# Gate and up products of two token blocks as seven block products instead of eight

## The reference

```python
g = jnp.einsum('bsd,edf->ebsf', h, Wg)          # e = 8 experts, d = 256, f = 1024
u = jnp.einsum('bsd,edf->ebsf', h, Wu)
expert_outs = jnp.einsum('ebsf,efd->ebsd', silu(g) * u, Wd)
expert_output = jnp.einsum('be,ebsd->bsd', gating_probs, expert_outs)
shared = jnp.einsum('bsf,fd->bsd', silu(h @ Sg) * (h @ Su), Sd)
return (1.0 - sg) * expert_output + sg * shared
```

## Time and profile before

| | |
|---|---|
| runs | 1375.63, 1377.25, 1380.95 us |
| profiled execution | span 1373.0 us; what lies around the span is not listed apart, the median of the runs is 4.25 us above the span |
| mean granted TensorE clock | 0.992 |
| busy in the span | PE 1346.5 us (98%), VectorE 755.6 (55%), ScalarE 329.8 (24%), GpSimd 45.7 (3%) |
| matmuls | 5832, of them 9 x 576 = 5184 in the experts and 384 in the GELU network |
| DMA | 39.6 MB, 29 GB/s over the span |

### The profile page before, as it was taken

One profiled execution on the slowest core, in us unless ns is written; L12 is line 12 of the kernel. 1 busy time (PEld: TensorE's weight loads), 2 busy tenths in 40 slices (PEclk: granted clock), 3 DMA queues, 4 the chain that ended last, 5 costly groups with the idle time before them and its releaser, 6 DMA issues.

```text
span 1373.0 us, 16497 instructions
## 1 busy us (share of the span) xinstructions
PE 1346.5 (98%) x5832; PEld 1079.9 (79%) x5832; DVE 755.6 (55%) x1231; ACT 329.8 (24%) x565; POOL 45.7 (3%) x48
## 2 busy tenths in 40 slices
PE   6799999999999999999999999999999999999998
PEld 4568888888888888888888888888888888888886
DVE  6956555555555555555555555555555555554444
ACT  2555622211112222111122221121222211111111
POOL 7500000000000000000000000000000000000000
PEclk8899999999999999999999999999999999999999
DMA  8020200000000000000000000000000000000000
GB/s 249 15 92 9 84 23 23 23 23 23 23 23 23 23 23 23 23 23 23 23 23 23 23 23 23 23 23 23 23 23 23 23 23 0 0 0 1 26 19 15
DMA packets 16432, 39.59 MB, mean 29 GB/s; under 512 B 6562, under 2 KB 9122, under 8 KB 16290
## 3 DMA queue, kind: packets, MB, share of 16 engines
q1 hardware_dynamic: 15536, 39.39, 8.8%
q10 hardware_dynamic: 882, 0.02, 0.0%
HBM read 37.31 MB, written 2.10 MB: 29 GB/s over the span
## 4 chain that ended last, share of the span: by engine, by line
PE 96%; DVE 3%; DMA 1%; ACT 0%; issue 0%; SPq 0%; DVEq 0%; ACTq 0%
PE ps L858 96%; DMA xT<-in_x_rows 1%; DVE x_dn L683 0%; DVE w_lo L713 0%; DVE gate L570 0%; DVE xT L609 0%; DVE poly L602 0%; DVE row_max L644 0%; DVE xT L729 0%; PE ps L875 0%; DVE denom L664 0%; DVE x_lo L721 0%; DVE x_dn L658 0%; DVE nb_all L595 0%; DVEq L45 0%
## 5 line engine op out<-in xcount | busy, mean ns | idle before, releaser
L858 PE MATMUL ps<-x_hi,w_hi 128*128 (+1 forms) x1216 | 480.7, 395 | 2.8 <-DVE x_lo L721 2.7
L858 PE MATMUL ps<-x_lo,w_hi 128*128 (+1 forms) x1216 | 480.7, 395 | 0.0
L858 PE MATMUL ps<-x_hi,w_lo 128*128 (+1 forms) x1216 | 477.4, 393 | 0.0
L828 DVE SCALAR_TENSOR_TENSOR hidden<-stage,gate,ps 128x512 f32<-128x512 f32 x288 | 215.3, 748 | 440.6 <-ACT stage L516 440.6
L516 ACT ACTIVATE stage<-ps 128x512 f32<-128x512 f32 x288 | 172.2, 598 | 928.3 <-PE ps L858 928.2
L858 PEld LDWEIGHTS ps<-x_hi,w_hi 128*128 128x128 f32 x1216 | 228.1, 188 | 60.1 <-issue 2.9
L858 PEld LDWEIGHTS ps<-x_hi,w_lo 128*128 128x128 f32 x1216 | 228.5, 188 | 54.3
L858 PEld LDWEIGHTS ps<-x_lo,w_hi 128*128 128x128 f32 x1216 | 228.2, 188 | 52.1
L858 PE MATMUL ps<-h_hi,w_hi 128*128 128x512 f32 x640 | 252.3, 394 | 0.0
L858 PE MATMUL ps<-h_lo,w_hi 128*128 128x512 f32 x640 | 251.9, 394 | 0.0
L858 PE MATMUL ps<-h_hi,w_lo 128*128 128x512 f32 x640 | 251.2, 392 | 0.0
(11 more groups left out here) (105 smaller groups left out, 286.2 us busy)
## 6 DMA issues: line engine op xcount, KB each, us to landing
raw<-in_moe_w SPq DMA_DIRECT2D x36, 768.0 KB, 4.3
out_x<-xT SPq DMA_DIRECT2D x8, 256.0 KB, 2.4
xT<-in_x_rows SPq DMA_DIRECT2D x2, 528.0 KB, 4.8
x_up<-in_x_rows SPq DMA_DIRECT2D x2, 520.0 KB, 6.6
x_dn<-in_x_rows SPq DMA_DIRECT2D x2, 520.0 KB, 10.0
raw<-in_fc_w SPq DMA_DIRECT2D x1, 1024.0 KB, 10.7
x_up<-in_x_rows SPq DMA_DIRECT2D x2, 504.0 KB, 9.3
x_dn<-in_x_rows SPq DMA_DIRECT2D x2, 504.0 KB, 11.8
```

What stands on the lines that cost most here:

```text
L828: nc.vector.scalar_tensor_tensor(hidden[:, k % PAIR, :], stage[:, k % PAIR, :], gate[:, ds(e, 1), ds(tb, 1)].rearrange("p e t -> p (e t)") ...
L858: return nc.tensor.matmul(out_ap, lhsT, rhs, start=first, stop=last)
```

## The change

A group is now one hidden chunk k and one round p of two token blocks (512 columns each). Gate and up for both blocks are the 2x2 block product of A = [[gate c0, gate c1], [up c0, up c1]] and B = [[x c0 of block 0, x c0 of block 1], [x c1 of block 0, x c1 of block 1]]. It is made in Winograd's form with seven block products. The sums S1 to S4 of weights (four 128x128 subtractions or additions a chunk, VectorE) and T1 to T4 of tokens (once, before the experts) are new. Down products stay as they were (four a group). PE issues 11 products of three matmuls a group: 33.

Partial sums are shared through PSUM. A11*B11 goes to bank A. ScalarE copies bank A into bank B (`seed`, PSUM to PSUM) and PE adds A12*B21 to A (gate of block 0) and S2*T2 to B. VectorE adds bank B and a ScalarE copy of S1*T1 (bank E, `p5_out`) and writes the sum back into bank E (`gate1_seed`), on which PE adds S4*B22 (gate of block 1). S3*T3 is added to B, VectorE sums B and the copy to the up of block 1 (`up1_sum`), and A22*T4 is added to B for the up of block 0. Bank B alternates between 6 and 7; the four down sums hold banks 0 to 3.

The gate value is applied once a round when the down sums are added to `xT`, and no longer to each hidden chunk. Both high parts of the hidden chunks are made on ScalarE. The weights come as 72 pieces (one chunk of one expert, six 128x128 blocks) through a ring of four raw slots; split weights lie in eight tiles, one per chunk, used by both rounds. The last three tiles take the place of the GELU network's weights. The experts are: the first written out, a loop over 1 to 7 with 16 groups in its body, the last written out. In the diff below the first `expert` is ScalarE's stream, the second VectorE's, and `group` is TensorE's.

```diff
+        A21, A11, A12, A22, D0, D1, S1, S2, S3, S4 = range(RT)
+        B11, B21, B22, T4, T1, T2, T3 = range(XT)
+        ROUNDS = 2
+        GROUPS = ROUNDS * FC
...
             with sp.Fori(1, E) as e:
-                for q in range(NT):
-                    sp.wait_ge(wlo_done, (e - 1) * (NT * PIECES) + (q + 1) * PIECES)
-                    sp.dma_start(raw[:, q * WQ:(q + 1) * WQ],
-                                 moe_w[ds(e, 1), :, q * WQ:(q + 1) * WQ].rearrange("e p w -> (e p) w")) \
-                      .then_inc(raw_in[q], 16)
+                for k in range(FC):
+                    sp.wait_ge(wlo_done, e * FC + k - RAWS + 1)
+                    piece_load(e, k)
...
+            def piece_high(e, k, after_round=True):
+                q = e * FC + k
+                act.wait_ge(wsum_done, 4 * q + 4)
+                if after_round:
+                    act.wait_ge(down0_done, (e - 1) * GROUPS + FC + k + 1)
+                nc.scalar.activation(w_hi[k][:, :, :], piece[:, k % RAWS, A11:RT, :], ACT.Copy).then_inc(whi_done, 1)
...
+            def seed(e, i):
+                n = e * GROUPS + i
+                act.wait_ge(p1_ps, n + 1)
+                if not starts(e, i, 2):
+                    act.wait_ge(hidden0_done, n - 1)
+                nc.scalar.activation(ps[:, BANK_B + i % 2, :], ps[:, BANK_A, :], ACT.Copy).then_inc(seeded, 1)
...
+            def expert(e, first, last):
+                for i in range(GROUPS):
+                    before = not starts(e, i, 1)
+                    seed(e, i)
+                    if before:
+                        hidden1_high(*earlier(e, i, 1))
+                    p5_out(e, i)
+                    gate0(e, i)
+                    if before:
+                        hidden0_high(*earlier(e, i, 1))
+                    gate1(e, i)
...
+                    elif i in (2, 3):
+                        piece_high(e, i + 4)
+                    elif i >= FC + 2 and not last:
+                        piece_high(e + 1, i - FC - 2)
...
+            def piece_sums(e, k):
+                w = [piece[:, k % RAWS, t, :] for t in range(RT)]
+                dve.wait_ge(piece_in[k % RAWS], (e * (FC // RAWS) + k // RAWS + 1) * 16)
+                done = 4 * (e * FC + k)
+                nc.vector.tensor_tensor(w[S1], w[A21], w[A22], ALU.add).then_inc(wsum_done, 1)
+                nc.vector.tensor_tensor(w[S3], w[A11], w[A21], ALU.subtract).then_inc(wsum_done, 1)
+                dve.wait_ge(wsum_done, done + 1)
+                nc.vector.tensor_tensor(w[S2], w[S1], w[A11], ALU.subtract).then_inc(wsum_done, 1)
+                dve.wait_ge(wsum_done, done + 3)
+                nc.vector.tensor_tensor(w[S4], w[A12], w[S2], ALU.subtract).then_inc(wsum_done, 1)
+
+            def piece_low(e, k):
+                dve.wait_ge(whi_done, e * FC + k + 1)
+                nc.vector.tensor_tensor(w_lo[k][:, :, :], piece[:, k % RAWS, A11:RT, :],
+                                        w_hi[k][:, :, :].bitcast(f32), ALU.subtract).then_inc(wlo_done, 1)
...
+            def gate1_seed(e, i):
+                n = e * GROUPS + i
+                dve.wait_ge(p6_ps, n + 1)
+                dve.wait_ge(p5_copied, n + 1)
+                nc.vector.tensor_tensor(ps[:, BANK_E, :], ps[:, BANK_B + i % 2, :], p5_copy[:, :],
+                                        ALU.add).then_inc(g1_seeded, 1)
...
+            def outputs_added(e, r, h):
+                done = (down0_done, down1_done)[h]
+                dve.wait_ge(done, (e * ROUNDS + r + 1) * FC)
...
+            def expert(e, first, last):
+                for i in range(GROUPS):
+                    before = not starts(e, i, 1)
+                    if before:
+                        hidden1_low(*earlier(e, i, 1))
+                        hidden0_mul(*earlier(e, i, 1))
+                    gate1_seed(e, i)
+                    if before:
+                        hidden0_low(*earlier(e, i, 1))
+                    if i % FC < 2 and not (first and i < FC):
+                        outputs_added(*((e, 0) if i >= FC else (e - 1, 1)), 1 - i % FC)
...
+                    elif 2 <= i <= 4:
+                        if i < 4:
+                            piece_sums(e, i + 4)
+                        piece_low(e, i + 3)
+                    elif i >= FC + 2 and not last:
+                        piece_sums(e + 1, i - FC - 2)
+                        if i > FC + 2:
+                            piece_low(e + 1, i - FC - 3)
+                    up1_sum(e, i)
+                    hidden1_mul(e, i)
...
+            def up0_end(e, i):
+                pe.wait_ge(u1_done, e * GROUPS + i + 1)
+                product(BANK_B + i % 2, i % FC, A22, i // FC, T4, False, True).then_inc(u0_ps, 1)
+
+            def group(e, i):
+                k, p = i % FC, i // FC
+                n = e * GROUPS + i
+                before, before2 = not starts(e, i, 1), not starts(e, i, 2)
+                if p == 0:
+                    pe.wait_ge(wlo_done, e * FC + k + 1)
+                if before:
+                    pe.wait_ge(silu0_done, n)
+                product(BANK_A, k, A11, p, B11, True, False).then_inc(p1_ps, 1)
+                if before:
+                    pe.wait_ge(silu1_done, n)
+                product(BANK_E, k, S1, p, T1, True, False).then_inc(p5_ps, 1)
+                if before:
+                    up0_end(*earlier(e, i, 1))
+                pe.wait_ge(seeded, n + 1)
+                product(BANK_A, k, A12, p, B21, False, True).then_inc(g0_ps, 1)
+                product(BANK_B + i % 2, k, S2, p, T2, False, False).then_inc(p6_ps, 1)
+                if before2:
+                    down(*earlier(e, i, 2), 0, 1)
+                if before:
+                    down(*earlier(e, i, 1), 1, 0)
+                    down(*earlier(e, i, 1), 1, 1)
+                pe.wait_ge(g1_seeded, n + 1)
+                product(BANK_E, k, S4, p, B22, False, True).then_inc(g1_ps, 1)
+                product(BANK_B + i % 2, k, S3, p, T3, False, False).then_inc(p7_ps, 1)
+                if before:
+                    down(*earlier(e, i, 1), 0, 0)
```

More of the change, by code:

```diff
@@ L1 @@
+import math
 import concourse.bass as bass
@@ L537, in _ @@
+            expert(0, True, False)
+            with act.Fori(1, E - 1) as e:
+                expert(e, False, False)
+            expert(E - 1, False, True)
+            hidden1_high(E - 1, GROUPS - 1)
+            hidden0_high(E - 1, GROUPS - 1)
         @block.vector
@@ new lines, in hidden0_low, with up1_sum @@
+            def hidden0_low(e, i):
+                n = e * GROUPS + i
+                dve.wait_ge(h0_hi_done, n + 1)
+                nc.vector.tensor_tensor(h0_lo[:, i % 2, :], hidden0[:, :], h0_hi[:, i % 2, :].bitcast(f32),
+                                        ALU.subtract).then_inc(h0_ready, 1)
+            def up1_sum(e, i):
+                n = e * GROUPS + i
+                dve.wait_ge(p7_ps, n + 1)
+                nc.vector.tensor_tensor(u_sum[:, :], ps[:, BANK_B + i % 2, :], p5_copy[:, :],
+                                        ALU.add).then_inc(u1_done, 1)
@@ L855, in _, with mm @@
+            expert(0, True, False)
+            with dve.Fori(1, E - 1) as e:
+                expert(e, False, False)
+            expert(E - 1, False, True)
+            hidden1_low(E - 1, GROUPS - 1)
+            hidden0_mul(E - 1, GROUPS - 1)
+            hidden0_low(E - 1, GROUPS - 1)
+            outputs_added(E - 1, 1, 1)
+            outputs_added(E - 1, 1, 0)
         @block.tensor
         def _(pe):
-            def mm(out_ap, lhsT, rhs, first, last):
-                return nc.tensor.matmul(out_ap, lhsT, rhs, start=first, stop=last)
+            def mm(out_ap, lhsT, rhs, first, last, seeded=False):
+                return nc.tensor.matmul(out_ap, lhsT, rhs, start=first, stop=last, skip_group_check=seeded)
@@ new lines, in _ @@
+            pe.wait_ge(xlo_done, XT)
+            pe.wait_ge(x2_summed, NT * DC)
+            for i in range(GROUPS):
+                if i == 1:
+                    pe.wait_ge(fc_summed, NT * DC)
+                if i == FC:
+                    pe.wait_ge(xlo_done, 2 * XT)
+                group(0, i)
+            with pe.Fori(1, E) as e:
+                for i in range(GROUPS):
+                    group(e, i)
+            e, i = E - 1, GROUPS - 1
+            up0_end(e, i)
+            down(e, i - 1, 0, 1)
```

517 lines of the change are left out of this document (305 added, 212 removed).

## The result

The changed kernel takes 1255.67 us (median of four runs, 1253.6 to 1256.92) against 1376.44 us for the kernel before (four runs, 1373.71 to 1380.95): a ratio of 0.912, 95% interval 0.910 to 0.914. 1283 us had been forecast, in a range of 1277 to 1308. The direction was right, and the gain of 120.8 us is nearly three tenths larger than the 93 to 94 us that were forecast.

The account below looks back on a forecast made before the run. TensorE's matmul count times pace was taken to bound the experts. Span 1373.0 - 100.1 + 2.0 + 1.8 + 0.5 + 1.8 = 1279.0 us; with the median run 4.25 above it, 1283 us, range 1277 to 1308.

Parts of the forecast that it names:

- 432 matmuls fewer, 432 x 0.2316: Experts: 33 matmuls instead of 36 in each of 144 groups, at an unchanged pace of 0.2316 us, saving 100.1 us.
- already run three to a bank at the same pace: Argument from the old kernel's down products against TensorE's pace worsening with three matmuls to a bank in turn.
- rival of a changed pace: TensorE's matmuls get slower with shared banks: 1318 us at 0.239 us each, 0.2527 gives all back; chance 0.04.
- The waits added: Handoffs between engines within a group: every wait met without weight work, margins from 0.43 us (seed) to 1.8 us.
- each further 0.1 us is 14 us: A chain step priced without a row and over 0.4 us dearer falls on all 144 groups.
- VectorE's weight work: Groups with sums and low part: VectorE cycle 6.9 us, under TensorE's 7.64, 0.15 late against a margin of 1.04.
- 17 instructions are in it: Rival: VectorE bounds weight groups if each instruction takes 0.04 us more; 1296 to 1300 us, chance 0.15.
- Beginning and end: TensorE's waits in the first two groups, 2.0 us together, and after S3 of the last group, 1.7 us.
- GELU stage: GELU network: VectorE gets up to 3.4 us of work per 2.78 us chunk three times; 0 to 2 us, 0.5 taken.
- Loop and table: Experts' loop: one table load counted at nothing, 1.8 us added for the longer body's instruction fetch.
- the loop head: Rival: VectorE or ScalarE stalls 2.4 to 4 us at the head in seven rounds; 1292 to 1303 us, chance 0.13.
- the clock: Rival: PSUM handoff gaps lower TensorE's granted clock, making it slower than before, 1385 to 1400 us or more; chance 0.04.

## Why the prediction was wrong

**The step that failed** is "432 matmuls fewer, 432 x 0.2316": not the count but the pace, which was carried over unchanged to the other 4752, as "a count of matmuls times a pace". The pace was 226.7 ns and not 231.7, which makes 24.0 us, the whole of the miss in the span (1279.0 forecast, 1255.1 measured). It lies in where the new arena puts the tiles, and the kernel before has the same gain from 480 bytes of padding (25.8 us for 5568 matmuls, 4.6 ns each). The new places were part of the change, but no step of the prediction asked what they do.

A sign of it stood in the trace of before. Between 184 and 1240 us one distance between starts in four is 0.24 us (in the changed kernel a single one is), with TensorE never waiting. The experts of the first weight slot (at 128, unlike the hidden chunks at 672) take 0.699 us for a down product, those of the second (at 672, like them) 0.688; and the last down products of the run, with no ups between them, take 0.68 each:
```profile
1366.12 0.39 PE L858 MATMUL ps<-h_hi,w_hi 128*128 128x512 f32 x1
...
1366.80 0.39 PE L858 MATMUL ps<-h_hi,w_hi 128*128 128x512 f32 x1
...
1367.48 0.39 PE L858 MATMUL ps<-h_hi,w_hi 128*128 128x512 f32 x1
```
The argument that downs "already run three to a bank at the same pace" averaged this away. The rival of a changed pace was on the list in one direction only; in the other, 0.4% was allowed for in the range, where 2.2% came.

That the rest of the sum comes out to 0.1 us is luck. The start of the network came 1.2 us earlier by chance, its stage was 3.4 us longer than forecast, 3.0 of them by the clock of that one execution, and the 1.8 us for the loop heads weren't needed.

**The waits added**: right. No wait of TensorE stands in the trace from 185 to 1240 us. The smallest margin, 0.43 us at the seed, was tested by dose: one more copy, 0.62 us, leaves TensorE waiting some 0.1 us, so the margin was 0.5 rather than 0.43. That copy costs 33 us, the next 92. The rule "each further 0.1 us is 14 us" held to within 5% (0.61 x 144 = 88).

**VectorE's weight work**: right in each price, and about right in the margin: 1.38 us more on each piece came out at 46 us in the experts, between the free 0 and the full 88. The rival's "17 instructions are in it" doesn't fit the cycle laid out above it, which lists 11; by these it would have taken 0.06 us on each to close the gap, not 0.04.

**Beginning and end**: 2.0 and 1.7 forecast, 1.8 and 1.8 us measured. At the beginning A12 starts 0.15 late and S4 0.96. The `up0_end` of the second group isn't late; A12 of the third is, by 0.29, as its seed copy stands in ScalarE's queue behind a high part that waited 1.19 us for VectorE's sums. The sum was right partly by luck: the waits were taken too large, and the 0.1 us after each wasn't counted. At the end the last `up0_end` starts 0.27 late, D1c0 0.70 and D0c0 0.50.

**GELU stage**: 0.5 forecast, 3.9 measured in the profiled execution, of which 3.0 are the clock, and 0.8 where the clock stayed up. The size was near, the path was not: VectorE's load was counted, but not that ScalarE's queue passes through it. A high part waits for the sums of its own chunk, and a GELU waits behind the high part. The padded kernel before takes 108.8 us for the stage, so by these executions, with tiles alike in both, the new work costs some 2.2 us, and the better places hide most of it.

**Loop and table**: 1.8 forecast, nothing measured. The one table load came where it was expected. Instruction packets did flow in the loop (stretch from 180 to 1240 us, against 2 of q8 in the earlier trace rows and 1 of q14 before):
```profile
q8 instruction: 8, 0.13, 0.0%
q14 instruction: 10, 0.08, 0.0%
```
No engine's stream shows a pause for them. The Trainium skill's page "Runtime: NRT & Kernel Launch", section "Instruction fetch mechanics", says that a taken branch out of the held pages forces a fetch first; more packets than before fit that, but TensorE's next group was never late.

**The rivals.** VectorE, the loop head and the clock all failed. The clock is 1.00 throughout the experts, and stays so with a wait in every group, in the kernel with three copies; from the GELU network on it fell only in that network's stage, in two stretches of about 3 us. The other side exists, 1380 us with a seed of three copies, but at a chain of 1.2 us more than the change has, and by plain waiting.

## What to carry to other kernels

When TensorE is busy 100% of a stage, count its matmuls, and then look at the distance between their starts, product by product. If like products differ with nothing waiting (here 0.68 to 0.70 us for three matmuls), place all tiles that feed it, weights and moving operands, high and low parts, at the same offset within 256 bytes, and time that before anything else. Look at the granted clock of a stage before the difference between two executions is put down to the code. Price a handoff by a chain from producer to the next product that needs it, with every instruction ahead of it in the in-order queues; an engine that is busy 70% of the time can be within one instruction of the bound in half of the groups.

## What the runs showed of the hardware

- Pace of 128x128 by 512-column float32r matmuls at full clock: 226.7 ns with all operands' tiles at the same place within 256 bytes (also when that place is 32 past a multiple of 64), 227.8 with the tokens' low parts alone 128 bytes off, 230.8 with the hidden chunks alone 32 off, 233 with all weights 32 or 128 bytes off. 256 and 512 bytes were tried with the tokens' low parts alone and cost nothing. By product of three matmuls: 0.680 us with all alike, 0.687 with one moving operand 128 off its weights, 0.700 with all of them off. Why unlike places cost time is not shown; these are offsets tried with one pattern of products.
- With 32 bytes between hidden chunks and weights, ups that read no moved tile are slower too, for about three products after the downs (0.693 to 0.697, then 0.685 us). With the tokens' low parts 128 bytes off, downs stay at 0.680.
- A matmul that had to wait is followed by one 0.1 us late (0.33 instead of 0.227 us from start to start), in each of the 51 groups looked at in the kernel with two seed copies.
- The granted clock fell to its lower level within a busy stage, for about 3 us at a time, in six of thirteen executions; a matmul then takes 0.43 us instead of 0.23 (94.6 to 97.6 us: clock 0.50).
- ScalarE copies 128x512 from PSUM to PSUM in 582 ns, and from PSUM to SBUF in 589. VectorE adding into PSUM takes 699 ns, into SBUF 687.
